# The last 128 tokens of a fused state-space and feed-forward layer: VectorE makes y, copies and layer norms in halves of d, and ready products stand earlier in TensorE's queue

## What is computed

```python
xn = x * rsqrt(mean(x * x) + 1e-6) * norm_w
xn = xn * sigmoid((xn @ select_proj_w.T + select_proj_b) * select_gate)
xp = xn @ x_proj_w.T                       # delta (128), B (128), C (128)
delta = softplus(xp[:128] @ dt_proj_w.T + dt_proj_b)
h = exp(delta_t * A) * h + (delta_t * xn_t) * B_t      # (2, 512, 128), for t in 0..1023
y_t = sum_n h * C_t
x = layernorm(x + (y + x * D_param) @ out_proj_w.T)
x = layernorm(x + (silu(x @ w_gate.T) * (x @ w_up.T)) @ w_down.T)   # hidden 2048
```

## Time and profile before

| | us |
|---|---|
| median of three runs | 2755.23 |
| lowest, highest | 2744.45, 2757.8 |
| the profiled execution, its own time | 2745.6 |
| its span, first to last instruction | 2743.8 |
| VectorE busy | 2605.7 (95%) |
| TensorE busy (matmul) | 2346.4 (86%) |
| ScalarE busy | 1540.3 (56%) |
| mean granted TensorE clock | 0.955 |

### The profile page before, as it was taken

One profiled execution on the slowest core, in us unless ns is written; L12 is line 12 of the kernel. 1 busy time (PEld: TensorE's weight loads), 2 busy tenths in 40 slices (PEclk: granted clock), 3 DMA queues, 4 the chain that ended last, 5 costly groups with the idle time before them and its releaser, 6 DMA issues.

```text
span 2743.8 us, 46936 instructions
## 1 busy us (share of the span) xinstructions
PE 2346.4 (86%) x17024; PEld 1290.3 (47%) x17024; DVE 2605.7 (95%) x4134; ACT 1540.3 (56%) x1957; POOL 844.9 (31%) x765
## 2 busy tenths in 40 slices
PE   4776677999779987899879997799978998899877
PEld 3322224555345543455435553455534554465557
DVE  2999999999999999999999999999999999999970
ACT  5554345664666555664556646566466655654733
POOL 2222222342324423343233433244232442243310
PEclk8999999999899999999989999999999999999988
DMA  3556665777657776677767786577766787688782
GB/s 131 207 208 217 218 231 208 262 278 272 240 201 280 278 259 234 222 279 280 264 211 242 277 286 241 205 271 270 269 241 217 276 279 261 237 295 300 258 324 91
DMA packets 192465, 673.65 MB, mean 246 GB/s; under 512 B 20976, under 2 KB 26096, under 8 KB 192240
## 3 DMA queue, kind: packets, MB, share of 16 engines
q1 hardware_dynamic: 152304, 544.81, 56.2%
q10 hardware_dynamic: 39936, 125.85, 13.5%
HBM read 662.18 MB, written 8.39 MB: 244 GB/s over the span
## 4 chain that ended last, share of the span: by engine, by line
DVE 51%; PE 22%; issue 17%; ACT 8%; DMA 1%; POOL 0%; ACTq 0%; POOLq 0%; DVEq 0%
DVE h L536 32%; DVE banks L526 19%; PE banks L796 7%; PE banks L928 5%; PE banks L942 3%; ACT a L745 3%; PE banks L905 2%; PE banks L875 1%; ACT L546 1%; PE banks L871 1%; DMA w_xp<-in_down_w 1%; PE banks L880 1%; DMA U<-in_xT 1%; ACT dt L582 0%; PE banks L872 0%
## 5 line engine op out<-in xcount | busy, mean ns | idle before, releaser
L745 ACT ACTIVATE a<-banks 128x2048 f32<-128x2048 f32 x512 | 961.3, 1878 | 861.6 <-PE banks L928 707.3
L536 DVE SCALAR_TENSOR_TENSOR h<-u_bc,BCt,banks 128x512 f32<-128x512 f32 x2048 | 1426.9, 735 | 15.4 <-PE banks L942 15.2
L526 DVE TENSOR_TENSOR banks<-a,h 128x512 f32<-128x512 f32 x2048 | 1326.4, 690 | 9.4 <-ACT a L745 9.4
L481 POOL TENSOR_TENSOR dexp<-spread,dt 128x512 f32<-128x512 f32 x512 | 539.7, 1054 | 1423.2 <-DVE banks L526 1353.2
L942 PE MATMUL banks<-h,cz 128*32 128x512 f32 x4096 | 714.7, 625 | 112.8 <-DVE h L536 111.8
L928 PE MATMUL banks<-dexp,A 32*128 32x256 f32 x8192 | 615.3, 416 | 125.0 <-ACT a L745 124.1
L928 PEld LDWEIGHTS banks<-dexp,A 32*128 32x128 f32 x8192 | 385.4, 192 | 460.4 <-ACT a L745 307.6
L796 PE MATMUL banks<-vT,w_ring 128*128 128x256 f32 x1792 | 446.7, 392 | 7.6 <-ACT up L714 6.9
L796 PEld LDWEIGHTS banks<-vT,w_ring 128*128 128x128 f32 x1792 | 322.0, 189 | 174.6 <-issue 118.2
L942 PEld LDWEIGHTS banks<-h,cz 128*32 128x32 f32 x4096 | 110.0, 109 | 402.9 <-issue 395.1
L905 PE MATMUL banks<-gated,w_ring 128*128 128x256 f32 x896 | 223.5, 392 | 8.9 <-ACT vT L719 6.7
(11 more groups left out here) (134 smaller groups left out, 1147.7 us busy)
## 6 DMA issues: line engine op xcount, KB each, us to landing
u_bc<-u_scratch SPq DMA_DIRECT2D x1024, 512.0 KB, 4.6
w_ring<-in_gu_w ACTq DMA_DIRECT2D x112, 512.0 KB, 5.3
w_ring<-in_down_w ACTq DMA_DIRECT2D x56, 512.0 KB, 5.4
a<-in_gu_w ACTq DMA_DIRECT2D x16, 512.0 KB, 6.8
U<-in_xT ACTq DMA_DIRECT2D x8, 512.0 KB, 6.4
u_scratch<-t_both ACTq DMA_DIRECT2D x16, 256.0 KB, 4.4
a<-in_down_w ACTq DMA_DIRECT2D x8, 512.0 KB, 4.2
x_tok<-in_x_rows SPq DMA_DIRECT2D x15, 256.0 KB, 6.1
```

Source lines behind the costliest of these rows:

```text
L481: e.tensor_tensor(dexp[:, q % E_RING, :, :, :], spread[:, :].unsqueeze(1).unsqueeze(1).to_broadcast(shape), by_step[:, :, first:first + BS ...
L526: e.tensor_tensor(m_ps[:, b, :], a[:, blk % A_RING, b, s, :], h[:, (t - 1) % H_RING, b * D:(b + 1) * D], ALU.mult).then_inc(s_m, 1)
L536: e.scalar_tensor_tensor(h[:, t % H_RING, part], u_bc[:, t % U_RING, part], BCt[c % 2][:, 0, b * TB + tl:b * TB + tl + 1], m_ps[:, b, :], ...
L745: e.activation(dst.rearrange("p b t (x j) -> p x (b t) j", j=GP), src.rearrange("p g (i r j) -> p (g i) r j", i=PAIR, j=GP), ACT.Exp, scal ...
```

## The change

Only the window behind the scan (x > LAST) is changed; all instructions of the scan stay as they are and in their order. There:

- VectorE adds y out of y_ps itself, in two halves of d; the last ScalarE copy to y_sb goes.
- yt and vt write their two halves into two banks (final_half: the unit's own bank, and half of one of the two banks of m_ps, which the scan no longer uses), and VectorE copies each half (ymc, vtc) as it comes.
- x_tok's product with the identity stands first in outp's bank, ahead of yt; w_out's first two blocks wait for the first copied half alone.
- The layer norms are bn_stats and bn_aggr on VectorE, Ln and Exp on one column on ScalarE (root_behind), and subtract-and-scale by VectorE in two halves out of the bank.
- Residual and transposes k = 0 to 2 of back stand ahead of the last quarter of down; only k = 3 waits for the last copy.

```diff
@@ vector
+            elif stage == "ya" and x > LAST:
+                e.wait_ge(s_xd, WINDOWS)
+                e.wait_ge(s_y, SEQ)
+                for i in range(2):
+                    part = slice(i * PAIR * P, (i + 1) * PAIR * P)
+                    rows = v(x, j)[:, part].rearrange("p (i g j) -> p g i j", i=PAIR, g=G)
+                    e.tensor_tensor(rows, rows, y_ps[:, part].rearrange("p (g i j) -> p g i j", i=PAIR, g=G), ALU.add
+                                    ).then_inc(s_y2, 1)
...
+        def final_window(e, x, stage, j):
+            parts = [slice(i * PAIR * P, (i + 1) * PAIR * P) for i in range(2)]
+            if stage == "ymc":
+                for i in range(2):
+                    e.wait_ge(s_yt2, i + 1)
+                    e.tensor_copy(ymodT(x, j)[:, parts[i]], final_half("yt", x, j, i)).then_inc((s_ym2, s_work)[i], 1)
+            elif stage in ("ln1", "ln2"):
+                n = int(stage == "ln2")
+                src = bank("back" if n else "outp", x, j)
...
+                e.bn_stats(moments[:, 0:6], src).then_inc(s_st, 1)
+                e.wait_ge(s_st, n + 1)
+                e.bn_aggr(moments[:, 6:8], moments[:, 0:6]).then_inc(s_ag, 1)
+                e.wait_ge(s_rt, 2 * (n + 1))
+                for i in range(2):
+                    e.tensor_scalar(v(x, j)[:, parts[i]], src[:, parts[i]], moments[:, 6:7], moments[:, 9:10],
+                                    ALU.subtract, ALU.mult).then_inc((s_nm, s_work)[i], 1)
+            elif stage == "vtc":
+                for i in range(2):
+                    e.wait_ge(s_vt2, i + 1)
+                    last = e.tensor_copy(vT_of(x, j)[:, PAIR * i:PAIR * (i + 1), :],
+                                         final_half("vt", x, j, i).rearrange("p (k t) -> p k t", k=PAIR))
+                last.then_inc(s_work, 1)
@@ scalar
+            def root_behind(stage, x, j):
+                n = int(stage == "ln2")
+                log_table()
+                e.wait_ge(s_ag, n + 1)
+                e.activation(moments[:, 8:9], moments[:, 7:8], ACT.Ln, bias=eps_ln[:, :]).then_inc(s_rt, 1)
+                e.wait_ge(s_rt, 2 * n + 1)
+                e.activation(moments[:, 9:10], moments[:, 8:9], ACT.Exp, scale=-0.5).then_inc(s_rt, 1)
+                if n:
+                    e.wait_ge(s_nm, 2)
+                    e.wait_ge(s_work, emptied("back", x, j))
+                    e.dma_start(out_rows[window_of(x, j)], v(x, j)).then_inc(d_out[j], 16)
...
-            window(WINDOWS - 1)
@@ tensor, yt and outp
+                    if x > LAST:
+                        e.wait_ge(d_xt[j], 16 * CHUNKS)
+                        e.matmul(bank("outp", x, j), ident[:, :], x_tok(x, j), start=True, stop=False)
...
+                    if x > LAST and not second:
+                        e.wait_ge(s_ym2, 1)
+                    else:
+                        e.wait_ge(s_work, emptied("yt", x, w))
@@ tensor, down
+                    if x > LAST and j == 4 * KB - 1:
+                        w = halves(x)[0]
+                        rows = bank("back", x, w)
+                        e.wait_ge(s_work, emptied("down", x, KB - 2))
+                        e.matmul(rows, ident[:, :], v(x, w), start=True, stop=False)
+                        for k in range(KB - 1):
+                            e.matmul(rows[:, k * P:(k + 1) * P], vT(x)[:, k, 0:P], ident[:, :], start=False, stop=False)
```

More of the change, by code:

```diff
@@ L226, in build @@
         stat = sb("stat", [P, 8])
+        moments = sb("moments", [P, 12])
         vT_all = sb("vT", [P, KB, 2, P])
@@ L364, in free, with final_half @@
             return turn
+        def final_half(stage, x, j, i):
+            return bank(stage, x, j)[:, 0:PAIR * P] if i == 0 else m_ps[:, ("yt", "vt").index(stage), 0:PAIR * P]
         def emptied(stage, x, j):
@@ L541, in vector @@
                     piece_behind(e, x, stage, j)
+                    final_window(e, x, stage, j)
         def scalar(e):
@@ L786, in scalar @@
                         before(x, stage, j)
-            window(WINDOWS - 1)
             for slot in sorted(plans[CHUNKS]):
                 for stage, x, j in plans[CHUNKS][slot]:
-                    behind(x, stage, j)
+                    if stage in ("ln1", "ln2"):
+                        root_behind(stage, x, j)
+                    elif stage not in ("ymc", "vtc"):
+                        behind(x, stage, j)
         def tensor(e):
@@ L866, in behind @@
                         e.wait_ge(d_wout, 16)
-                    e.wait_ge(s_work, emptied("yt", x, w))
-                    if second:
+                    if x > LAST and not second:
+                        e.wait_ge(s_ym2, 1)
+                    else:
+                        e.wait_ge(s_work, emptied("yt", x, w))
+                    if x > LAST:
+                        for k in (2 * second, 2 * second + 1):
+                            last = e.matmul(dst, ymodT(x, w)[:, k * P:(k + 1) * P], w_out[:, k, :], start=False, stop=k == 3)
+                        if second:
+                            last.then_inc(s_outp, 1)
+                    elif second:
                         e.wait_ge(d_xt[w], 16 * (min(x, LAST) + 1))
@@ L876, in behind @@
                 elif stage == "vt":
-                    dst = take(stage, x, j)
-                    e.wait_ge(s_ln, 6 * (norms["ln1", x, j] + 1))
+                    dst = bank(stage, x, j) if x > LAST else take(stage, x, j)
+                    if x <= LAST:
+                        e.wait_ge(s_ln, 6 * (norms["ln1", x, j] + 1))
                     for k in range(KB):
-                        last = e.matmul(dst[:, k * P:(k + 1) * P], v(x, j)[:, k * P:(k + 1) * P], ident[:, :], start=True,
+                        if x > LAST and k == 0:
+                            e.wait_ge(s_nm, 1)
+                        elif x > LAST and k == PAIR:
+                            e.wait_ge(s_work, emptied("outp", x, j))
+                        part = dst if x <= LAST else final_half(stage, x, j, k // PAIR)
+                        at = k if x <= LAST else k % PAIR
+                        last = e.matmul(part[:, at * P:(at + 1) * P], v(x, j)[:, k * P:(k + 1) * P], ident[:, :], start=True,
                                         stop=True)
-                    last.then_inc(s_vt, 1)
+                        if x > LAST and k % PAIR:
+                            last.then_inc(s_vt2, 1)
+                    if x <= LAST:
+                        last.then_inc(s_vt, 1)
                 elif stage == "gu":
@@ L908, in behind @@
                 elif stage == "back":
-                    dst = take(stage, x, j)
+                    dst = bank(stage, x, j) if x > LAST else take(stage, x, j)
                     e.wait_ge(s_work, emptied("down", x, KB - 1))
-                    e.matmul(dst, ident[:, :], v(x, j), start=True, stop=False)
+                    if x <= LAST:
+                        e.matmul(dst, ident[:, :], v(x, j), start=True, stop=False)
                     first = P * halves(x).index(j)
-                    for k in range(KB):
+                    for k in range(KB) if x <= LAST else (KB - 1,):
                         last = e.matmul(dst[:, k * P:(k + 1) * P], vT(x)[:, k, first:first + P], ident[:, :], start=False,
```

19 lines of the change are left out of this document (16 added, 3 removed).

## The result

| | before | after |
|---|---|---|
| median of six runs, us | 2754.26 (2744.45 to 2757.8) | 2735.66 (2733.25 to 2739.75) |
| the profiled execution, its own time | 2745.6 | 2733.25 |
| its span | 2743.8 | 2731.5 |

The ratio is 0.994, with a 95% interval of 0.9921 to 0.9958: faster by 12 to 22 us, 16.5 in the middle. The medians are 18.6 us apart.

What follows compares the result with a forecast made beforehand. After E, the end of the last y row, one dependent chain of 77.7 us was taken as the bound. Gains of 9.1 + 4.85 + 0.1 + 2.7 = 16.8 us off median 2755.2 gave 2738.4 us, range 2726 to 2742.6.

Steps and rivals of the forecast that it cites:

- Term 1: From the last y row to the end of w_out's products: 14.64 us falls to 5.55, gain 9.1 us.
- Term 2: From w_out's end to the first gate/up pass: gain 4.3 us at full clock, 3.3 at half.
- Term 3: TensorE's clock in gate/up's 256 passes: up to 2.1 us to be had, half counted, 1.05.
- Term 4: Last transposes, from down's end: 2.45 us falls to 2.3, gain 0.1 us, bounds 0 and 0.5.
- Term 5: Last layer norm, last transpose to the store: 5.08 us falls to 2.4, gain 2.7 us.
- A: Rival: the clock already falls in front of w_out; gain only 11.85 us, 2743.4 us; chance 0.08.
- B: Rival: layer-norm table loads are not hidden; gain 13.3 to 14.2 us, about 2741.5 us; chance 0.08.
- C: Rival: clock stays at half through gate/up and down, slower, 2781 us; chance 0.02.
- D: Rival: halves run one after the other, w_out stays at half clock; gain 9 us, 2746 us; chance 0.05.
- The signs: Expected in the changed profile's end: w_out's end +5.5, first gate/up +9.3 to 10.3, gate/up 28.7 to 30.8 us.

Runs made afterwards that it cites:

- beforewarm: Kernel before the change, with 44 identity products filling TensorE's four pauses; last y row to end of span 71.05 us, against 77.66 without them.
- acty: Changed kernel with ScalarE again copying the last y and VectorE adding it from there in halves; last y row to end 65.20 us, against 61.81.
- backold: Changed kernel with residual and all four transposes back behind the wait for down's last copy; start of down to last transpose 16.70 us, against 16.69.
- best: Changed kernel plus nine fillers, residual and three transposes behind down's last quarter, four tiles loaded later, last norm's subtract-and-scale whole; median 2732.83 us, ratio 0.9921.
- again: The changed kernel unaltered, run once more beside the kernel before; median 2737.54 us against 2752.69, ratio 0.994.
- late: Changed kernel with residual and three transposes behind down's last quarter instead of ahead; start of down to last transpose 16.06 us, against 16.69.
- tiles: Changed kernel with the last window's first four gate/up tiles loaded four scan steps later; last y row to end 63.17 us, against 61.81.
- xtokold: Changed kernel with x_tok's product behind w_out again; last y row to the end of both products 6.56 us, against 5.79.

## Why the prediction was right

2735.66 us measured, 2738.4 forecast; by the profiled executions, from E on, 15.85 us gained for 16.8. The terms, with what each measured:

- Term 1, 9.1 forecast, **8.85 measured** (14.64 - 5.79). VectorE's halves of y are hidden under x_tok's product, the clock stayed full, w_out started at +2.10 for +2.05. The passes take 3.69 us for 3.5; eight at the prediction's own 0.43 would be 3.44 and end at +5.49, so its +5.55 is 0.06 over its terms, without weight. The split stood too: the clock's share 3.8 (beforewarm) for 3.9, the late copy 3.3 (acty) for 2.8.
- Term 2, 4.3 at full clock, **4.11 measured**. bn_stats 0.71 us and bn_aggr 0.19 lay in their bounds. The subtract-and-scale takes 0.55 us for its first half, not 0.42, which was the row of a product of two tensors.
- Term 3: half of 2.1 us forecast, **0.43 measured**. A fall was called likelier than not and came, just ahead of the first gate/up pass. Taking half of the clock's gain was a mean over two cases, not a size: gate/up takes 28.8 us or 30.3 to 31.5, and nothing between. So the term stood for neither case, and the one that came lay 0.6 us from it. Terms 2 and 3 together gave 4.54 us for 4.85.
- Term 4, 0.1 forecast, **0.07 measured**, and nothing against backold. That ready products ahead of the wait buy only what the wait would hold was right.
- Term 5, 2.7 forecast, **2.44 measured**. The store came at +2.63, not +2.4, by the two halves of 1.00 us that I had at 0.8. The issue of the store to the end of the span took 2.52 us for 2.46, which no term had.
- The rivals: A (clock down in front of w_out) didn't come in any execution of the change, but a fall as early came in acty and best, where TensorE paused. It cost 1.65 us there in w_out's passes (acty) and 0.97 ahead of them (best), not 3.4, since the clock was back before w_out's passes were through, or before they began. B: no. The last table load runs from 2725.82 to 2727.10 and Ln starts at 2727.33, 0.04 us behind VectorE's bn_aggr, with 0.23 us free behind the load. The drain that the Trainium skill (ScalarE: Activation LUTs, What ACT_TABLE_LOAD costs) adds to a switch of set would have put Ln at about 2728.5, an estimate (2727.10 + 1.38). This trace does not show it. VectorE's product of 128x256 out of SBUF (L450) takes 0.42 us, and its add of the same size out of y's bank (L459) 0.42 too. The Trainium skill (VectorE: DVE Perf Modes, The TRN2 errata) has a higher fixed cost for a bank, an estimate of 0.06 us; these rows don't show it. C and D: no. The waits are met half by half, and the clock came back after 3.4 us.
- The signs: w_out's end at +5.79 (5.5 said), the first gate/up pass at +9.65 and gate/up's 30.32 us lie where they were said to. The 6.3 us from down's end to the store, with the moved products in front, don't follow from the prediction's own terms: 2.3 + 2.4 = 4.7, and 5.6 with the last eight passes of down, which stand behind the moved products. Measured were 5.92 (2723.06 to 2728.98).
- The tail gave 0.95 us less than forecast, the median 1.8 us more: 18.6. That the median still came close is in part luck: the 2.75 us between 15.85 and 18.6 made up for what the tail lacked, and I put them down to the scan's spread, which no run here separates out. E alone moved by 4.5 us between after and again, and again's medians are only 15.15 us apart.

## What to carry to other kernels

Where one chain of waits ends a kernel, count from the event at which it begins. Executions differed here by 11 us before that event, and behind it, for the same steps, by the clock's 1.5 us and hundredths. Split an instruction in halves only where someone waits for the first half. A product that is ready earlier than it is needed belongs into a wait of TensorE: behind the product whose result another engine is about to copy, and not ahead of it (16.06 us for 16.69). And where TensorE pauses ahead of a long run of products, products without use in the pause can pay: in the kernel before they gave 6.6 us with nothing else changed.

## What the runs showed of the hardware

- With all else equal gate/up took 28.82 us (late) or 30.32 (after, again), by whether the granted clock fell to 0.50 around pauses of 2.1 and 0.6 us with 1.2 us of transposes between them. Nine filler products of 0.11 us a pass cost nothing that can be seen (to w_out and to gate/up 5.81 and 9.66 for 5.79 and 9.65).
- Four 512 KB loads ahead in ScalarE's queue made the next one land 16.9 us after its issue (2636.65 to 2653.52) instead of within 7.5 (tiles). Whether the queue's order or the DMA engines, busy throughout (share 1.03 from 2645 to 2653.5), held it up, the runs don't separate.
- Eight transposing passes take 1.05 us back to back; their first four took 0.46 us from the end of another product and 0.70 after a pause, at the same clock (after, xtokold).
